# Last two expert tiles added by selection products, K and V weights behind the last gate, barrier out

## The reference

```python
xn = _layernorm(x, axis=-1)
s = _L0_attn_ref(xn, ...)                  # xn + scan(...) @ out_proj_w
g = _silu(_L0_ffn_ref(xn, ...))            # y = sum over e of comb[:, e] * (h_e @ proj_w[e].T)
x = x + s * g
xn = _layernorm(x, axis=-1)
s = _L1_attn_ref(xn, Wq, Wk, Wv, Wo)
g = _silu(_L1_ffn_ref(xn, ...))
return x + s * g
```

## Time and profile before

| | |
|---|---|
| median of three runs | 779.48 us |
| the profiled execution | 780.78 us, its span 779.0 us |
| PE busy | 706.5 us, 91% |
| DVE, ACT, POOL busy | 477.7, 417.9, 399.3 us |
| mean granted TensorE clock | 0.968 |
| DMA | 96.21 MB, mean 124 GB/s |

### The profile page before, as it was taken

How to read it: one execution, slowest core, us unless ns; L and a number is a source line. 1 busy time by engine, 2 the same in 40 slices (tenths; PEclk the granted TensorE clock), 3 DMA queues, 4 the chain that set the end, 5 groups by cost and what they waited for, 6 DMA issues and landing times.

```text
span 779.0 us, 13360 instructions
## 1 busy us (share of the span) xinstructions
PE 706.5 (91%) x4536; PEld 618.6 (79%) x4536; DVE 477.7 (61%) x1023; ACT 417.9 (54%) x1043; POOL 399.3 (51%) x451
## 2 busy tenths in 40 slices
PE   2999999999999991388889999999999999999995
PEld 2887989989989981266678888888888888888874
DVE  7582644423323445485566787777877778777764
ACT  4446244233233234236467776677766777667663
POOL 1412442332332220326777776787767877677460
PEclk9899999999999996599899999999999999999999
DMA  5075877778787505235224323322233222232001
GB/s 187 28 253 186 280 251 249 237 253 254 248 254 250 171 15 155 41 116 147 82 69 117 67 62 69 89 69 64 65 69 89 71 58 67 58 89 56 1 1 54
DMA packets 101859, 96.21 MB, mean 124 GB/s; under 512 B 50592, under 2 KB 72032, under 8 KB 101664
## 3 DMA queue, kind: packets, MB, share of 16 engines
q1 hardware_dynamic: 99584, 89.33, 39.6%
q0 software_dynamic: 2208, 6.03, 2.2%
HBM read 69.24 MB, written 9.31 MB: 101 GB/s over the span
## 4 chain that ended last, share of the span: by engine, by line
PE 64%; DVE 10%; POOL 9%; ACT 8%; issue 6%; SPq 1%; POOLq 1%; DMA 1%; DVEq 0%; ACTq 0%
PE bank L1631 15%; PE bank L1491 8%; PE bank L1665 8%; PE bank L1492 8%; PE bank L1493 8%; PE bank L1487 6%; POOL prob L1449 5%; ACT prob L1264 3%; PE bank L1752 3%; DVE nmax L1010 2%; PE bank L1753 2%; POOL q_lo L1461 2%; ACT kv_hi L1271 2%; DVE o_lo L1023 1%; POOL wq_lo L1429 1%
## 5 line engine op out<-in xcount | busy, mean ns | idle before, releaser
L1449 POOL TENSOR_TENSOR prob<-prob,rinv 128x128 f32<-128x128 f32 (+3 forms) x256 | 177.6, 724 | 102.1 <-DVE rinv L1015 102.1
L1264 ACT ACTIVATE prob<-bank,nmax 128x512 f32<-128x512 f32 (+3 forms) x256 | 133.2, 528 | 45.4 <-DVE nmax L1010 43.9
L1019 DVE TENSOR_TENSOR kv_lo<-bank,kv_hi 128x512 fp32r<-128x512 f32 x160 | 110.0, 687 | 52.7 <-ACT kv_hi L1271 51.8
L1271 ACT ACTIVATE kv_hi<-bank 128x512 fp32r<-128x512 f32 x160 | 96.3, 602 | 78.7 <-PE bank L1487 78.6
L1631 PEld LDWEIGHTS bank<-xgT,wm 128*128 128x128 f32 x920 | 108.1, 192 | 5.3 <-issue 3.8
L1631 PE MATMUL bank<-xgT,wm 128*128 128x128 f32 x920 | 110.3, 275 | 0.5 <-ACT xgT L1173 0.5
L1487 PE MATMUL bank<-cst,prob 128*128 128x128 f32 x640 | 97.8, 276 | 3.0 <-POOL prob L1449 1.2
L1010 DVE TENSOR_REDUCE nmax<-bank 128x1 f32<-128x512 f32 (+2 forms) x192 | 91.1, 502 | 10.8 <-PE bank L1755 10.2
L1491 PE MATMUL bank<-kv_hi,v_lo 128*128 128x128 f32 (+3 forms) x256 | 93.2, 364 | 0.3 <-DVE kv_lo L1019 0.3
L1752 PE MATMUL bank<-kT,qT 128*128 128x512 f32 (+3 forms) x256 | 81.6, 324 | 11.2 <-ACT prob L1264 7.2
L912 DVE TENSOR_TENSOR hE<-sil,bank 128x512 f32<-128x512 f32 x23 | 15.8, 688 | 111.0 <-PE bank L1631 80.5
(11 more groups left out here) (301 smaller groups left out, 1479.0 us busy)
## 6 DMA issues: line engine op xcount, KB each, us to landing
wm<-in_w_moe SPq DMA_DIRECT2D x23, 1280.0 KB
wm<-in_w_moe SPq DMA_DIRECT2D x23, 640.0 KB, 5.7
qT<-q_hi SPq DMA_DIRECT2D x124, 64.0 KB, 2.0
qT<-q_lo SPq DMA_DIRECT2D x124, 64.0 KB, 2.0
k_exp<-k_rows SPq DMA_DIRECT2D x56, 64.0 KB, 2.0
wtl<-in_w_moe_tail SPq DMA_DIRECT2D x46, 64.0 KB
gy<-y_rows SPq DMA_DIRECT2D x8, 256.0 KB, 4.8
wq_raw<-in_w_qkv SPq DMA_DIRECT2D x32, 64.0 KB, 2.5
```

What stands on the lines that cost most here:

```text
L1019: TT(p_lo[:, b_, :], bank[2 + b_ % 2][:, :], p_hi[:, b_, :].bitcast(F32), ALU.subtract).then_inc(plo_done, 1)
L1264: ins = actv(prob[:, i % 2, h, POFF[j]:POFF[j] + (j + 1) * P], bk[:, at:at + (j + 1) * P], ACT.Exp, bias=nmax[:, i % 2, h, j:j + 1], accum ...
L1271: actv(p_hi[:, b_, :], bank[2 + b_ % 2][:, :], ACT.Copy).then_inc(phi_done, 1)
L1449: ins = GT(seg, seg, rinv[:, i % 2, k, j:j + 1].to_broadcast([P, (j + 1) * P]), ALU.mult)
```

## The change

The list:

- POOL scatters tiles 0 to 20 only. The chunks start 11.5 units apart instead of 12, and the last chunk's O stands 12.7 units behind its start. New entries: two `pick` on DVE, four `sum` on DVE (after H3, P and L of the end, ahead of the scaling of tile 22), one `kv` on ACT and on POOL.
- `pick` compares each row's token, less 128 times the tile's number, with the lane number: for tiles 21 and 22 it gives a 0/1 matrix of 128 x 128 for each of the 8 token tiles.
- `rows` scales tiles 21 and 22 into an upper part `y_up` and a lower part `y_low`, both on chip.
- `sum` adds the two read-back rows of a token, in place, where xs and gate of the first batch lay; the rows are read after tile 20's scatter has landed, after the first four chunks are projected, and behind the K and V loads.
- `sum_pair` on PE brings that sum into a PSUM bank by one product with the identity matrix, and adds eight selection products (two tiles, two token tiles, upper and lower). SiLU and the product with the scan's result work in PSUM.
- Rows of `y_rows` that no scatter writes any more must be zero: SP writes 2 MB of zeros at the start, and POOL's first fetch and ACT's gates wait for that.
- K and V weights go to the ring slot that tile 20 leaves free; SP loads them once tile 20's row product is done. ACT and POOL split them at the end of their lists. SP loads the first q weights after the last chunk is projected, and the o weights and further K weights after the last pair is summed.
- `end_phase` goes; waits for the tables, the K and V weights, and the last row product take its place.

```diff
-            z += [(at + 3.1, "PE", "P", j - 1), (at + 3.2, "DVE", "P", j - 1), (at + 3.3, "POOL", "P", j - 1)]
+            z += [(at + 3.1, "PE", "P", j - 1), (at + 3.2, "DVE", "P", j - 1)]
+        if 0 < j <= NJ - PICKED:
+            z += [(at + 3.3, "POOL", "P", j - 1)]
...
+    z += [(4 * NJ + 0.5, "ACT", "kv", 0), (4 * NJ + 0.6, "POOL", "kv", 0)]
+    z += [(4 * NJ + 0.1 * n, "DVE", "sum", n) for n in range(NT // 2)]
+    z += [(42.6 + 6 * i, "DVE", "pick", i) for i in range(PICKED)]
...
-        o = a + 9.5
+        o = a + (9.5 if c + 1 < NT else 12.7)
...
-CHUNK_AT = [3 + 12 * c for c in range(NT)]
+PICKED = 2
+CHUNK_AT = [3 + 11.5 * c for c in range(NT)]
...
+MIXED_IN = (6, 7, 5, 3)
...
+        y_up = Map(tiles.at - sized([P, 2, C], F32))("y_up", [P, 2, C], F32R)
+        y_low = Map(both.at)("y_low", [P, XR, C], F32R)
...
-        gy = back("gy", [P, 2, NT, C])
-        gate_y = back("gate_y", [P, NT, C])
...
+        def gy(k, n):
+            return (xs, gate)[k][:, n, 0:HALF]
+        def gate_y(n):
+            return bank[MIXED_IN[n]][:, :].rearrange("p (t c) -> p t c", c=C)
...
+            sp.wait_ge(ones_ready, 3)
+            sp.dma_start(y_rows[0:2 * T, :].rearrange("(a p) c -> p a c", p=P),
+                         zeros.unsqueeze(1).to_broadcast([P, 2 * T // P, C])).then_inc(xn_out, 16)
...
-            sp.wait_ge(row_full, NJ)
+            sp.wait_ge(row_full, NJ - 2)
+            for c in range(KC):
+                for h in range(2):
+                    load_wk(0, c, h, wk0[:, c, h * P:(h + 1) * P])
+                sp.dma_start(wv0[:, c, :].rearrange("p (g d) -> p g d", d=HD),
+                             w_qkv[:, :, c, (GQ + 1) * HD:(GQ + 2) * HD].rearrange("g p d -> p g d")).then_inc(kv_in, 16)
...
-                sp.wait_ge(row_out[u], (NJ + 1 - u) // 2 * 16)
+                sp.wait_ge(row_out[u], (NJ - PICKED + 1 - u) // 2 * 16)
+            sp.wait_ge(s_part, TB)
...
-                    sp.dma_start(gy[:, k, 2 * n:2 * n + 2, :], yv[:, k, 2 * n:2 * n + 2, :]).then_inc(pair_in[n], 16)
...
-            end_phase(sp)
+                    sp.dma_start(gy(k, n).rearrange("p (t c) -> p t c", c=C), yv[:, k, 2 * n:2 * n + 2, :]).then_inc(pair_in[n], 16)
+            sp.wait_ge(s_part, NT)
...
+            sp.wait_ge(mixed, NT // 2)
...
-                TS(y_row[:, j % 2, :], bank[3][:, 0:C], tab[:, 2, j:j + 1], None, ALU.mult).then_inc(row_taken, 1)
+                weight = tab[:, 2, j:j + 1]
+                if j < NJ - PICKED:
+                    TS(y_row[:, j % 2, :], bank[3][:, 0:C], weight, None, ALU.mult).then_inc(row_taken, 1)
+                else:
+                    dve.wait_ge(xg_full, NJ - PICKED)
+                    TS(y_up[:, j % 2, :], bank[3][:, 0:C], weight, None, ALU.mult).then_inc(y_hi_done, 1)
+                    dve.wait_ge(y_hi_done, NT + PICKED + 1 + j - NJ)
+                    STT(out=y_low[:, (j - PICKED) % XR, :], in0=bank[3][:, 0:C], scalar=weight, in1=y_up[:, j % 2, :].bitcast(F32),
+                        op0=ALU.mult, op1=ALU.subtract).then_inc(row_taken, 1)
+            def pick(i):
+                j = NJ - PICKED + i
+                then(TS(spare_f[:, 0:NT], edges[:, 0:NT], -1.0, tab[:, 1, j:j + 1], ALU.mult, ALU.add))
+                TT(picks[:, i, :, :], lane_no.unsqueeze(1).to_broadcast([P, NT, P]),
+                   spare_f[:, 0:NT].unsqueeze(2).to_broadcast([P, NT, P]), ALU.is_equal).then_inc(table_ready, 1)
...
+                elif op == "pick":
+                    pick(n)
+                elif op == "sum":
+                    dve.wait_ge(pair_in[n], 32)
+                    TT(gy(0, n), gy(0, n), gy(1, n), ALU.add).then_inc(table_ready, 1)
...
-            def mixed_pair(n):
-                dve.wait_ge(pair_in[n], 32)
-                ts = slice(2 * n, 2 * n + 2)
-                TT(gate_y[:, ts, :], gy[:, 0, ts, :], gy[:, 1, ts, :], ALU.add).then_inc(mixed, 1)
             def add_pair(n):
-                xt2, g2 = x_tok[:, 2 * n:2 * n + 2, :], gate_y[:, 2 * n:2 * n + 2, :]
+                xt2 = x_tok[:, 2 * n:2 * n + 2, :]
...
-                dve.wait_ge(s_part, 2 * n + 2)
-                then(TT(g2, g2, s_tok[:, 2 * n:2 * n + 2, :], ALU.mult))
-                TT(xt2, xt2, g2, ALU.add).then_inc(x_ready, 1)
+                dve.wait_ge(s_part, NT)
+                then(TT(gate_y(n), gate_y(n), s_tok[:, 2 * n:2 * n + 2, :], ALU.mult))
+                TT(xt2, xt2, gate_y(n), ALU.add).then_inc(x_ready, 1)
...
-            mixed_pair(0)
-            mixed_pair(1)
...
-                if n + 2 < NT // 2:
-                    mixed_pair(n + 2)
...
-            end_phase(dve)
...
+                elif op == "kv":
+                    act.wait_ge(kv_in, 96)
+                    actv(wk0[:, :, :], wk0[:, :, :], ACT.Copy, scale=HD ** -0.5).then_inc(k_scaled, 1)
+                    actv(wv0_hi[:, :, :], wv0[:, :, :], ACT.Copy)
+                    act.wait_ge(k_scaled, 1)
+                    actv(wk0_hi[:, :, :], wk0[:, :, :], ACT.Copy).then_inc(w_hi_done, 1)
...
-            act.wait_ge(turns_full, 1)
...
+            for n in range(NT // 2):
+                act.wait_ge(mixed, n + 1)
+                actv(gate_y(n), gate_y(n), ACT.Silu).then_inc(gated, 1)
+                if n == 1:
+                    act.wait_ge(turns_full, 1)
+                if n > 0:
+                    ins = actv(turns[:, n - 1, :], bank[n - 1][:, :], ACT.Copy)
...
+            actv(sv[:, 8, :], ones[:, 0:NT], ACT.Sqrt)
...
-            for n in range(NT // 2):
-                act.wait_ge(mixed, n + 1)
-                actv(gate_y[:, 2 * n:2 * n + 2, :], gate_y[:, 2 * n:2 * n + 2, :], ACT.Silu).then_inc(gated, 1)
-            actv(sv[:, 8, :], sv[:, 0, :], ACT.Sqrt)
...
-            end_phase(act)
...
+                elif op == "kv":
+                    gp_.wait_ge(w_hi_done, 3)
+                    GT(wv0_lo[:, :, :], wv0[:, :, :], wv0_hi[:, :, :].bitcast(F32), ALU.subtract)
+                    GT(wk0_lo[:, :, :], wk0[:, :, :], wk0_hi[:, :, :].bitcast(F32), ALU.subtract).then_inc(w_lo_done, 1)
...
-            gp_.wait_ge(w_hi_done, 3)
...
-            end_phase(gp_)
+            gp_.wait_ge(row_full, NJ)
...
+            def sum_pair(n):
+                dst = bank[MIXED_IN[n]]
+                pe.wait_ge(table_ready, 4 + PICKED + n + 1)
+                mm(dst[:, :], ident, gy(0, n), start=True, stop=False)
+                for i in range(PICKED):
+                    j = NJ - PICKED + i
+                    pe.wait_ge(row_taken, j + 1)
+                    for t in range(2):
+                        to = dst[:, t * C:(t + 1) * C]
+                        mm(to, picks[:, i, 2 * n + t, :], y_low[:, (j - PICKED) % XR, :], start=False, stop=False)
+                        ins = mm(to, picks[:, i, 2 * n + t, :], y_up[:, j % 2, :], start=False, stop=i == PICKED - 1 and t == 1)
+                ins.then_inc(mixed, 1)
+            pe.wait_ge(xend_ready, NT)
+            pe.wait_ge(y_ready, NT)
+            sum_pair(0)
+            sum_pair(1)
...
+            pe.wait_ge(s_part, NT)
+            sum_pair(2)
+            sum_pair(3)
...
-            end_phase(pe)
...
+            pe.wait_ge(turns_ready, 1)
...
+            pe.wait_ge(w_lo_done, 4)
+            pe.wait_ge(turns_ready, 2)
...
```

More of the change, by code:

```diff
@@ L264, in layered_kernel @@
         assert first.at <= weights_at
-        w_out_sb = Map(weights_at)("w_out_sb", [P, NCH, C])
+        w_out_sb = Map(top_at - NCH * C * 4)("w_out_sb", [P, NCH, C])
+        picks = Map(hT_at + 2 * KC * T * 4)("picks", [P, PICKED, NT, P], F32R)
+        zeros = gate[:, 0, 0:C]
         table = Map(both.at)
@@ L307, in layered_kernel @@
         assert tiles.at <= hT_at + 2 * KC * T * 4
+        y_up = Map(tiles.at - sized([P, 2, C], F32))("y_up", [P, 2, C], F32R)
+        y_low = Map(both.at)("y_low", [P, XR, C], F32R)
         weights = Map(weights_at)
-        wm = weights("wm", [P, 3, FULL, WM])
         wtl = weights("wtl", [P, 3, KC, P])
         ptl = weights("ptl", [P, 3, C])
-        back = Map(weights_at)
-        gy = back("gy", [P, 2, NT, C])
-        gate_y = back("gate_y", [P, NT, C])
+        wm = weights("wm", [P, 3, FULL, WM])
+        def gy(k, n):
+            return (xs, gate)[k][:, n, 0:HALF]
+        def gate_y(n):
+            return bank[MIXED_IN[n]][:, :].rearrange("p (t c) -> p t c", c=C)
+        kv_at = weights.at - FULL * WM * 4
+        assert (NJ - 3) % 3 == 2
+        raw, lower, upper = Map(kv_at), Map(kv_at), Map(kv_at + 3 * KC * HALF * 2)
+        wk0, wv0 = raw("wk0", [P, KC, 2 * P]), raw("wv0", [P, KC, KVH * HD])
+        wk0_lo, wv0_lo = lower("wk0_lo", [P, KC, 2 * P], F32R), lower("wv0_lo", [P, KC, KVH * HD], F32R)
+        wk0_hi, wv0_hi = upper("wk0_hi", [P, KC, 2 * P], F32R), upper("wv0_hi", [P, KC, KVH * HD], F32R)
+        assert raw.at <= kv_at + 3 * KC * HALF * 2 and upper.at <= top_at
         last = Map(top_at - 3 * 2 * KC * KVH * HD * 4)
[L316 to L319, removed]
```

(21 more changed lines are left out.)

20 lines of the change are left out of this document (4 added, 16 removed).

## The result

| kernel | median us | against before, 95% interval |
|---|---|---|
| before | 780.3 (4 runs beside it) | |
| after | 772.74 (771.76 to 774.21, 4 runs) | 0.9909, 0.9881 to 0.9936 |

The change makes the kernel 7.6 us faster; 8.9 were predicted. The profiled execution of after took 774.21 us, its span is 772.4, the mean granted clock 0.982: 6.6 us less than the profiled execution of before.

The account below looks back on a forecast made before the run. PE bounds the expert stage; the gain lies in the 29.87 us of waits behind it. 10.9 gained less 1.0 stalls, 0.8 clock, 0.2 start gives 8.9: 771.9 us profiled, 770.6 against the median; range 765.5 to 775.

Parts of the forecast that it names:

- The place and the mechanism: Last row product to normalised rows: without the barrier wait (L434), 19.0 us long instead of 29.87, 10.9 gained.
- Tp: The prediction's time mark: the end of the last row product in the expert stage, 292.55 us before the change.
- Stalls of the expert stage: Expert stage: PE waits ahead of the output products of chunks 3 and 5, 1.0 us in all, bounds 0 and 2.5.
- Sums and hold: Pair sums on DVE: POOL's weight split holds DVE operations with two SBUF inputs; sums end Tp + 4.95, otherwise Tp + 3.5.
- Reads: Reads of scattered rows: first at about Tp - 6.7, pairs landing at Tp - 3.2 to + 2.9.
- Rival 2: Reads late through small packets or the scatter behind the weights: pairs 3 us later, 773.7 us; chance 0.15.
- Tail: Last pair's gate, product, sum and statistics: last statistics start at Tp + 16.0, normalised rows at Tp + 19.0.
- Clock: PE's pair sums: a dip of the granted clock costing 1.6 us at even odds, 0.8 charged; bounds 0 and 4.
- 1 (no meeting of POOL and DVE): Pair sums: POOL's split early or DVE winning turns, sums at Tp + 3.5, no clock dip, 768.4 us; chance 0.22.
- Rival 3: Clock dip in the pair sums and zeros at the start, both at their bounds: 2.5 to 3 us more, 773.4; chance 0.10.
- Rival 4: Expert stage: PE waits for POOL's line in seven shifted chunks, up to 4.6 us each, 32 us: 803; chance 0.03.
- Rival 5: Between the layers: some other wait of the same length stands behind the barrier, 778 us; chance 0.04.

Follow-up runs that it names:

- split_behind_sums: The kernel after, with POOL taking the lower parts of the K and V weights only when DVE has done its four pair sums: 771.92 us.
- barrier_back: The kernel after, with the barrier of five engines put back in front of the last statistics: 773.81 us.
- before_no_barrier: The kernel before, with only the barrier between the layers replaced by single waits, nothing else of the change: 775.41 us.
- all_scattered: chunks_12 with all 23 tiles scattered and read back, without picks, split of the last rows or selection products: 776.97 us.
- turns_in_gap: chunks_12 with table turns directly behind the last row product, ACT's upper q weights ahead of the root, POOL's K/V split behind the pair sums: 764.17 us.
- chunks_12: The kernel after, with chunks 12 units apart again and the pair sums behind tile 22's scaling in DVE's list: 768.79 us.
- drift_only: The kernel after, with the first seven chunks 11.9 units apart instead of 11.5 and the last chunk where it was: 770.78 us.

## Why the prediction was nearly right

*The place and the mechanism* were right: Tp to the normalised rows lost L434 and went from 29.9 to 18.55 us (19.0 predicted), and the gain lies in it alone.

*Stalls of the expert stage: the step that failed.* The sum had 1.0 us for late chunks, and nothing between the row products 21 and 22. Drift cost 3.0 and the bank wait 1.2, 4.2 in place of 1.0. I had found the right place (chunk 3, POOL's line, 0.73 against 0.5), but I priced only the one or two lines that came out late, each by itself. A stall moves all that follows against the other engines, and short waits don't show as idle time. PE's busy share of the stage was 98.8%, so the sign that I had named for drift, less than 98%, did not show it either. The wait for bank 3 was readable before: with Y moved ahead, P(21) and P(22) are neighbours, both write bank 3, and the new scaling is two operations of 0.48 us.

*Sums and hold.* DVE and POOL met as forecast: 2.85 for the lower half of y, 1.77 for one sum, each ending 0.55 us behind POOL. The sums ended at Tp + 3.3, not + 4.95, since the lower half of y could start at Tp - 3.05 and not at Tp - 1.6: the wait for bank 3 delays Tp, but not the work that doesn't depend on row product 22. For the same reason pair 0 was done at Tp + 5.0 instead of 6.55, and the last pair's statistics started at Tp + 14.6 instead of 16.0. One cause thus stands in two terms with opposite signs, and of the 4.39 us that Tp is late some 1.4 were not on the path of the sums.

*Reads.* SP needed 3.4 us for the K and V loads, not 5.7. DVE never waited for a read in after; the last landed near Tp + 0.5 (from split_behind_sums) instead of + 2.9. Rival 2, late reads, is out. My Tp - 6.7 for the first read was also worked out wrongly: it is the mean of two times that must both have passed, so the later, Tp - 6.3, was due.

*Tail.* From the start of the last pair's statistics to the rows 3.0 us were expected and 3.95 measured: the operation held by POOL's memset before is free, but another is held by the subtraction for q, 1.05 us. I had the row for such a hold and didn't look for who would stand beside it in the new order.

*Clock.* No dip in the pair sums: 0.8 us charged in vain. PE's gaps there are of 1.2 us at most. *Start*: 0.2 charged, nothing measured. *Pick*: 1.23 us for 1.15. So the 8.9 us of the forecast become, in the profiled executions, 8.9 less 3.4 (stage, 4.4 for 1.0) and 0.35 (from the rows to the end), plus 0.45 (between, 18.55 for 19.0), 0.8 and 0.2: 6.6, which is the difference of the spans. That the total came so close is partly luck: without the 1.45 us of errors the other way these 2.3 us of miss would be 3.75.

*Rivals.* 1 (no meeting of POOL and DVE) is refuted by the trace; split_behind_sums shows it would have been worth 1.8 us, where I had 1.45 and the dip. Rival 3 had the size but not the cause. Rival 4, drift that costs more than the change gains, was the right mechanism at a smaller size: 3.0 us and not 32. Rival 5: barrier_back and before_no_barrier show that only half of the barrier's 7.45 us came free by itself, since POOL's split, memsets and subtraction for q stood behind it; the early loads had to clear the first two out of the way.

## What to carry to other kernels

Before a barrier is removed, ask what the engines that arrive last will do beside the freed one: here POOL's split, memsets and subtraction took back half of it. When a list of interleaved work is re-spaced, price the whole stage by running the old spacing as a control: the gain of 11.3 us between the layers was bought with 4.4 us in a stage that had been without idle time, and nearly all of it came back with the old spacing. Work that depends on nothing (table turns) belongs where the engine waits, not ahead of work that is ready.

## What the runs showed of the hardware

- DVE operations of 8 to 512 elements whose inputs all lie in SBUF were held by POOL's two-input subtraction: 8 elements 1.22 us instead of 0.17, 512 elements 2.85 instead of 0.68, and in all_scattered one state update of 512 elements 3.95, in the time of POOL's split of both weights. POOL's side is stretched too: 1.73 us for 512 elements that take 1.27. Not held were a TENSOR_TENSOR with one input in PSUM (`bank<-bank,sT`, 0.70 us at 296.78 in turns_in_gap, inside POOL's subtraction of 295.14 to 297.52) and a RECIPROCAL of 8 elements (0.20 us at 313.12 in before_no_barrier, inside that of 312.78 to 314.04).
- POOL's memsets held a small TENSOR_SCALAR, which took 0.56 us before and 1.63 in before_no_barrier instead of 0.17, but neither the lower half of y (0.68 in chunks_12) nor the sums beside them in after (three in 1.88 us from 298.34, memsets from 297.81 to 299.72).
- The granted clock stayed at 2.4 GHz (1.00) from 292.9 to 307.0, where PE was 83% busy with gaps of up to 1.2 us, and stood at 1.2 GHz (0.50) for the 3.6 us of turns that followed 7.9 us of idle PE.
- A write of 2 MB of zeros from one on-chip tile landed 14.1 us after issue, beside the load of the first weights, and moved nothing: ACT's split of w_in starts at 10.50 us (10.52 before).
- The first expert product starts near 64.7 us in six profiled executions and near 66.4 in five, with kernels that are alike up to there but for the zeros. The clock makes the difference: in after the products of 512 columns start 0.43 us apart until about 34 us and 0.23 apart from there, in drift_only the change comes near 31.6. Why it comes earlier in some is open.
